# The skip of a Mamba-2 recurrence on VectorE and GpSimd instead of TensorE, the state's decay ahead of the next chunk's products, and other places for TensorE's product steps

## The reference

```python
# graph part of layer 0
msg = layernorm(x) @ W + B
sens = exp(-(1.0 / adj - 1.0) ** 2 / 0.5)
x = x + where(adj < 1.0, sens, 0.0) @ msg
# feed-forward part of layer 0: a Mamba-2 block on layernorm(x), 8 heads of 64, state 64
z, xBC, dt = split(x @ W_in);  xBC = silu(conv4(xBC) + conv_b);  xh, Bm, Cm = split(xBC)
dt = softplus(dt + dt_bias);   A = -exp(A_log)
h[t] = exp(dt[t] * A) * h[t-1] + dt[t] * outer(xh[t], Bm[t])       # per head
Y[t] = h[t] @ Cm[t] + xh[t] * D[:, None]                            # the last term is the skip
Y = Y * silu(z);  Y = Y * rsqrt(mean(Y * Y) + EPS) * norm_w
x = x + (Y @ W_out) @ W_lin + b_lin
```

## Time and profile before

| | us |
|---|---|
| median of three runs (2358.29 to 2360.41) | 2358.39 |
| span of the profiled execution | 2358.5 |
| TensorE busy (share of the span) | 2189.1 (93%) |
| VectorE busy | 1803.0 (76%) |
| ScalarE busy | 1566.7 (66%) |
| GpSimd busy | 1146.6 (49%) |
| mean granted TensorE clock | 0.979 |

### The profile page before, as it was taken

How to read it: one execution, slowest core, us unless ns; L and a number is a source line. 1 busy time by engine, 2 the same in 40 slices (tenths; PEclk the granted TensorE clock), 3 DMA queues, 4 the chain that set the end, 5 groups by cost and what they waited for, 6 DMA issues and landing times.

```text
span 2358.5 us, 26231 instructions
## 1 busy us (share of the span) xinstructions
PE 2189.1 (93%) x8900; PEld 1393.1 (59%) x8900; DVE 1803.0 (76%) x2083; ACT 1566.7 (66%) x2541; POOL 1146.6 (49%) x928
## 2 busy tenths in 40 slices
PE   7999999999999999989999999998999987787998
PEld 4544545555555556456766666676766664444886
DVE  5666767777777765324999998999989998996665
ACT  5577686777686845425676767677676868775444
POOL 2101322222231313213988888888988888890000
PEclk9999999999999999999999999999999999898999
DMA  6243332323232323233323232323323221312121
GB/s 234 72 134 102 108 116 90 125 96 122 87 125 88 119 90 134 83 107 109 131 93 125 90 125 89 117 99 107 117 100 125 90 83 43 117 36 98 36 81 45
DMA packets 117495, 241.22 MB, mean 102 GB/s; under 512 B 8770, under 2 KB 66370, under 8 KB 116978
## 3 DMA queue, kind: packets, MB, share of 16 engines
q1 hardware_dynamic: 108290, 207.14, 26.4%
q0 software_dynamic: 8528, 31.36, 3.8%
q10 hardware_dynamic: 544, 1.05, 0.1%
HBM read 219.20 MB, written 20.32 MB: 102 GB/s over the span
## 4 chain that ended last, share of the span: by engine, by line
PE 65%; ACT 10%; POOL 10%; DVE 10%; issue 5%; DMA 0%; ACTq 0%; DVEq 0%; POOLq 0%
PE ps L685 13%; PE ps L727 10%; POOL dB L2306 6%; PE ps L971 5%; DVE h L1473 3%; PE ps L849 2%; PE ps L823 2%; PE ps L955 2%; POOL acc L2288 2%; PE ps L709 2%; ACT ps L1659 2%; ACT L1657 1%; POOL du L2302 1%; PE ps L755 1%; PE ps L753 1%
## 5 line engine op out<-in xcount | busy, mean ns | idle before, releaser
L1473 DVE TENSOR_TENSOR_SCAN h<-ps,hst,dB 128x512 f32<-128x512 f32 x512 | 636.9, 1270 | 59.0 <-ACT ps L1659 50.5
L2306 POOL TENSOR_TENSOR dB<-du,bc 128x512 f32<-128x512 f32 x512 | 648.0, 1287 | 61.6 <-DVE h L1473 59.1
L685 PE MATMUL ps<-wgt,msg 128*128 128x512 f32 x1024 | 489.0, 598 | 2.1 <-DVE xb L1181 2.1
L1659 ACT ACTIVATE ps<-dt,cols 128x512 f32<-128x512 f32 x512 | 351.9, 692 | 181.1 <-DVE h L1473 178.8
L727 PE MATMUL ps<-raw,msg 128*128 128x256 f32 x1792 | 436.3, 379 | 0.9 <-ACT hb L1659 0.9
L971 PE MATMUL ps<-consts,h 128*128 128x128 f32 x2048 | 318.9, 281 | 70.7 <-DVE acc L1435 38.0
L971 PEld LDWEIGHTS ps<-consts,h 128*128 128x128 f32 x2048 | 251.6, 144 | 224.8 <-DVE acc L1435 73.4
L727 PEld LDWEIGHTS ps<-raw,msg 128*128 128x128 f32 x1792 | 324.0, 190 | 74.1 <-issue 42.1
L685 PEld LDWEIGHTS ps<-wgt,msg 128*128 128x128 f32 x1024 | 190.0, 192 | 206.2 <-issue 204.6
L1659 ACT ACTIVATE wgt<-wgt 128x1024 f32<-128x1024 f32 x256 | 257.9, 1046 | 51.9 <-DVE wgt L1146 50.5
L2288 POOL TENSOR_TENSOR acc<-acc,part 128x512 f32<-128x512 f32 x174 | 226.4, 1301 | 59.7 <-ACT part L1659 58.3
(11 more groups left out here) (320 smaller groups left out, 3589.9 us busy)
## 6 DMA issues: line engine op xcount, KB each, us to landing
raw<-in_adjT SPq DMA_DIRECT2D x256, 512.0 KB, 3.4
bc<-tmp_bc SPq DMA_DIRECT2D x64, 512.0 KB, 4.6
E<-tmp_bc POOLq DMA_DIRECT2D x32, 512.0 KB, 4.1
xb<-in_xT POOLq DMA_DIRECT2D x8, 512.0 KB, 4.1
tmp_x<-xb POOLq DMA_DIRECT2D x8, 512.0 KB, 4.2
x<-tmp_x SPq DMA_DIRECT2D x8, 512.0 KB, 5.8
tmp_x<-x SPq DMA_DIRECT2D x8, 512.0 KB, 4.8
msg<-in_W SPq DMA_DIRECT2D x4, 1024.0 KB, 10.6
```

The lines of the kernel that those rows point to most:

```text
L685: x = e.matmul(P[d][:, :], msg[:, j, d * 128:(d + 1) * 128], wgt[g % NW][:, l, :], start=j == 0, stop=j == NJ - 1)
L1473: e.tensor_tensor_scan(hr[n % 3][:, m, :], PS[4 + k % 2].t[:, :], dBr[k % 4][:, :], hst[:, n % 16, m:m + 1], ALU.mult, ALU.add).then_inc(S ...
L1659: return e.activation(out, in_, func, bias=bias, scale=scale)
L2306: e.tensor_tensor(dBr[k % 4][:, :], du[:, m, :], bcr[i % 3][:, n % 2, :], ALU.mult).then_inc(S("dB"), 1)
```

## The change

- The skip leaves TensorE. The four matmuls by diagD of each chunk are gone; the products with E now start the bank Y. In `inner(s)` VectorE first multiplies the transposed x tile X by a row of D spread over all partitions (`Drow`) into a new tile `skips[s % 2]`; in `outer(s)` GpSimd adds tmp to it (semaphore skip), and VectorE's last sum reads skips instead of tmp.
- Drow is made once, near 37 us: one more matmul on TensorE (a matrix of ones by diagD) and a copy on VectorE. diagD now shares the memory of skips[0], and the bias row Bbc that of skips[1]; the rows are loaded by two DMAs instead of one, and both are waited for.
- GpSimd's decay of the state (`carried`) no longer opens `outer(s)`. It stands in `inner(s + 1)`, ahead of xdec and of the product E for that chunk; for the last chunk it opens `outer`.
- FILLS puts 23 instead of 16 product steps at named places, and 7 fewer are spread. In the part quoted above TensorE's stream now reads: layernorm, transposes(0), p6, transposes(1), p, layernorm, p7, L745, Yo(0), p, St(0), p, Y(0), p, xbc0, p, transposes(2), p, xbc0, p2, z0, Yo(1), p, z0, St(1), sums, p, xbc1.
- The last stage counts two events on one semaphore (b2c) instead of two.

```diff
-        rows = sb(cA, "rows", [128, NROW])
-        Bbc, dtb, Abc = rows[:, 0:256], rows[:, 256:288], rows[:, 288:296]
-        diagD = sb(cA, "diagD", [128, 4, 128])
+        rows = sb(cA, "rows", [128, NROW - D])
+        dtb, Abc = rows[:, 0:32], rows[:, 32:40]
+        Drow = sb(cA, "Drow", [128, 512])
...
+        skip0 = sb(cA, "skip0", [128, 512])
...
+        skips = [skip0, sb(cA, "skip1", [128, 512])]
+        diagD = skip0[:, :].rearrange("p (m c) -> p m c", m=4)
...
-        FILLS, SEND, WFIRST, WLAST, EVAC, PREND = ((5, 3), (7, 2), (8, 2), (25, 2), (30, 2), (38, 2), (50, 2), (57, 1)), 58, 0.04, 0.925, 0.97, 0.95
+        FILLS, SEND, WFIRST, WLAST, EVAC, PREND = ((5, 3), (7, 2), (8, 3), (25, 2), (30, 2), (32, 2), (38, 4), (50, 3), (57, 2)), 58, 0.04, 0.925, 0.97, 0.95
...
-                    w.wait_ge(S("setup"), 5)
                     w.wait_ge(Y.evac, Y.n - 1)
-                    for m in range(4):
-                        e.matmul(Y.ps[:, m * 128:(m + 1) * 128], cc[:, m, ts_], diagD[:, m, :], start=m == 0, stop=False,
-                                 skip_group_check=True)
                     yield
                     w.wait_ge(S("M"), 4 * ib + s + 1)
                     w.wait_ge(X.evac, X.n)
                     for h in range(8):
-                        i = e.matmul(Y.ps[:, h * 64:(h + 1) * 64], Es[:, h, :], xd[:, h * 64:(h + 1) * 64], start=False,
-                                     stop=h == 7, skip_group_check=True)
+                        i = e.matmul(Y.ps[:, h * 64:(h + 1) * 64], Es[:, h, :], xd[:, h * 64:(h + 1) * 64], start=True,
+                                     stop=True)
...
+                    b = drow_use()
+                    w.wait_ge(S("setup"), 5)
+                    w.wait_ge(b.evac, b.n - 1)
+                    e.matmul(b.ps[:, :], one, skip0[:, :], start=True, stop=True).then_inc(b.full, 1)
...
+                    if c < 2:
+                        w.wait_ge(drow_use().evac, drow_use().n)
+                    e.tensor_tensor(skips[s % 2][:, :], X.ps[:, :], Drow[:, :], ALU.mult)
                     e.tensor_tensor(heads(xd[:, :]), heads(X.ps[:, :]), dt[:, 8 * s:8 * s + 8, None].broadcast_to([128, 8, 64]),
                                     ALU.mult).then_inc(X.evac, 1)
...
                     w.wait_ge(Y.full, Y.n)
-                    w.wait_ge(Yo.evac, Yo.n)
-                    e.tensor_tensor(tmp[:, :], tmp[:, :], Y.ps[:, :], ALU.add).then_inc(Y.evac, 1)
+                    w.wait_ge(S("skip"), c + 1)
+                    e.tensor_tensor(tmp[:, :], skips[s % 2][:, :], Y.ps[:, :], ALU.add).then_inc(Y.evac, 1)
...
+                    b = drow_use()
+                    w.wait_ge(b.full, b.n)
+                    e.tensor_copy(Drow[:, :], b.ps[:, :]).then_inc(b.evac, 1)
...
-            e.dma_start(rows[:, :], t["rows"].broadcast_to([128, NROW])).then_inc(S("d_rows"), 16)
+            e.dma_start(rows[:, :], t["rows"][:, D:NROW].broadcast_to([128, NROW - D])).then_inc(S("d_rows"), 16)
+            e.dma_start(Bbc[:, :], t["rows"][:, 0:D].broadcast_to([128, D])).then_inc(S("d_rows"), 16)
...
                     yield
+                    if s:
+                        carried(s - 1)
                     w.wait_ge(X.evac, X.n)
...
-                def outer(s):
+                def carried(s):
                     if s:
                         w.wait_ge(outer_use(ib, s - 1, 1).evac, outer_use(ib, s - 1, 1).n)
...
                     e.tensor_tensor(heads(hd[:, :]), heads(h0[0:64, :]), ecd[0:64, 2, s, :, None].broadcast_to([64, 8, 64]),
                                     ALU.mult).then_inc(S("hd"), 1)
-                    yield from [None] * 5
+
+                def outer(s):
+                    yield from (None, None)
+                    Yo = outer_use(ib, s, 0)
+                    w.wait_ge(Yo.evac, Yo.n)
+                    e.tensor_tensor(skips[s % 2][:, :], skips[s % 2][:, :], tmp[:, :], ALU.add).then_inc(S("skip"), 1)
+                    yield from (None, None, None)
```

More of the change, by code:

```diff
@@ L219, in build @@
         hd = sb(cA, "hd", [64, 512])
+        skip0 = sb(cA, "skip0", [128, 512])
+        cM = ExitStack()
+        Bbc = sb(cM, "Bbc", [128, D])
+        cM.close()
+        skips = [skip0, sb(cA, "skip1", [128, 512])]
+        diagD = skip0[:, :].rearrange("p (m c) -> p m c", m=4)
         cA.close()
@@ L283, in message_use @@
             if ib % 2:
-                return ring_b.use(ib // 2 * 6 + (4 if ib > 1 else 0) + i)
+                return ring_b.use(ib // 2 * 6 + (5 if ib > 1 else 0) + i)
             return ring_a.use(ib // 2 * 6 + i)
@@ L288, in combined_use, with drow_use @@
             return ring_b.use(6 + m)
+        def drow_use():
+            return ring_b.use(10)
         def pre_use(ib, i):
@@ L436, in build @@
         over_a = [(prod[1].use(NB).full, prod[1].use(NB).n), (ssd_use(NB - 1, 27).evac, ssd_use(NB - 1, 27).n), (ssd_use(NB - 1, 31).evac, ssd_use(NB - 1, 31).n),
-                  (S("hd"), 4 * NB), (S("M"), 4 * NB), (S("xdec"), 4 * NB), (S("halo"), NB + 1),
+                  (S("hd"), 4 * NB), (S("M"), 4 * NB), (S("skip"), 4 * NB), (S("xdec"), 4 * NB), (S("halo"), NB + 1),
                   *((S(f"d_x2_{b}"), 16 * len(range(b, NB, 3))) for b in range(3)), (S("d_m2"), 16 * (NB - 2))]
@@ L1087, in mean_of_bias @@
                 b = end_use(2)
-                w.wait_ge(S("b2c"), 1)
+                w.wait_ge(S("b2c"), 2)
                 w.wait_ge(b.evac, b.n - 1)
@@ L1134, in messages @@
                 yield
-                w.wait_ge(S("d_rows"), 16)
+                w.wait_ge(S("d_rows"), 32)
                 for s in range(4):
@@ L1138, in messages @@
                     w.wait_ge(b.full, b.n)
-                    e.tensor_tensor(msg[:, 4 * ib + s, :], b.ps[:, 0:256], Bbc, ALU.add).then_inc(b.evac, 1)
+                    e.tensor_tensor(msg[:, 4 * ib + s, :], b.ps[:, 0:256], Bbc[:, :], ALU.add).then_inc(b.evac, 1)
                     yield
@@ L1574, in second_matrices @@
                 w.wait_ge(b_tw.evac, b_tw.n)
-                e.tensor_scalar(b2[:, 0, :], b2[:, 0, :], tw[:, 0:1], None, ALU.mult).then_inc(S("b2a"), 1)
-                w.wait_ge(S("b2a"), 1)
+                e.tensor_scalar(b2[:, 0, :], b2[:, 0, :], tw[:, 0:1], None, ALU.mult).then_inc(S("b2c"), 1)
+                w.wait_ge(S("b2c"), 1)
                 e.scalar_tensor_tensor(b2c[:, :], b2[:, 1, :], tw[:, 1:2], b2[:, 0, :], ALU.mult, ALU.add).then_inc(S("b2c"), 1)
@@ L2217, in ssd @@
                         yield from inner(s + 1)
+                    else:
+                        carried(s)
                     yield from outer(s)
```

2 lines of the change are left out of this document (1 added, 1 removed).

## The result

| | before | after |
|---|---|---|
| median of the runs | 2358.34 us | 2380.64 us (2376.35 to 2382.33, 4 runs) |
| ratio | | 1.0087, 95% interval 1.0075 to 1.0099 |
| profiled span, mean granted clock | 2358.5 us, 0.979 | 2374.3 us, 0.973 |

A forecast was written before the change was run, and what follows sets the result against it. TensorE was taken to bound steady blocks (busy 110.2 of 112.4 us). Start +1.8, six blocks -7.0, seventh -2.4 and eighth -3.0 sum to -10.6 us, from 2358.39 to 2347.8; range 2332 to 2357.

The forecast's parts named there:

- forecast at 19.1 us: Second xbc group: TensorE arrives 19.1 us after the dt matmuls instead of 22.6, then waits for ScalarE's z copy.
- I take 0.6: Block start: VectorE's new product makes the normalised input late, so the dt matmuls at L745 start 0.6 us later.
- the upper bound of 1.9: Block start: the loss at L745 if the early decay on GpSimd also fell on VectorE's L1146 pair, 1.9 us.
- between 0 and 0.75 us later: First y of a block: VectorE's product with z, which ScalarE awaits, is done 0 to 0.75 us later.
- two meetings on GpSimd: First y: skip sum beside the L1146 pair, costing VectorE 0.2 to 1.3 us, and E beside L1153, possibly 2.4.
- waits until 592.95 to 593.7: Second xbc group: TensorE arrives at 591.6, waits for the z copy, starts 0.75 to 1.5 us earlier than before.
- 1.1 of gain: Steady block: wins 0.75 to 1.5 us, taken as 1.1, of the 3.56 us that TensorE saves.
- The clock: Blocks: granted clock was 1.00 despite 1.14 us idle spells; a fall would make the prediction wrong altogether; no chance given.
- Forecast 5.4 us for the two blocks: Last two blocks, where TensorE has idle time: 2.4 us won in the seventh and 3.0 in the eighth.
- the start 0.7 instead of 1.8: Kernel start: one more matmul and VectorE's copy cost 0.9 to 2.2 us, taken as +1.8.
- The 0.45 us a chunk: Eighth block: decay and update leave the chunk's cycle and the skip sum enters, a gain of 0.45 us a chunk.
- the third was nearest: Rival: VectorE and the shared access become the bound, up to 7.5 us a block against 3.56 saved; 2371 us, chance 0.10.

The follow-up runs named there:

- the new places alone: The kernel before the change with only the changed kernel's places for the product steps; 2359.61 us (0.9994 to 1.0013).
- no sum: The changed kernel without GpSimd's skip sum, VectorE's product still made but unused; median 2370.09 us, ratio 1.0037 to 1.007.
- the split with old places: The changed kernel with chunks 0 and 1's skip on TensorE, decay behind E, earlier z copy, product steps placed as before the change; 2360.77 us.

## Why the prediction was wrong

**What held.** TensorE's saving is 3.56 us a block. Its arrival at the second xbc group, forecast at 19.1 us behind the dt matmuls, was 19.24 (22.57 less the wait of 3.33). The limit there is ScalarE's z copy. The state's update no longer waits for the decay.

**The block start (step: "I take 0.6").** The product's part was right, 0.68 us, but it is the product of chunk 1, the second transpose group. What failed is the reason by which I set the upper bound of 1.9 aside: that the decay comes up while the second half of the VectorE pair is already running. It came up about then (459.69, while the second half was recorded as running from 459.40) and got in all the same. The dt matmuls waited 1.90 us, which is that bound; the decay alone costs 1.3 (1.29 in the kernel before, 1.30 in the one without skip).

**The first y (step: "between 0 and 0.75 us later").** It comes 1.46 us later, counted from dt matmuls that are 1.90 late themselves. The loss needs both the early decay and the sum, on whichever engine the sum stands: with the decay late y is 0.28 later, without the sum 0.09 earlier, with the sum on VectorE 1.47 later. I had counted two meetings on GpSimd and left out the third, the decay of the next chunk, which the edit puts beside the pair ahead of y (472.73 beside 471.23). A moved instruction has a new neighbour in every chunk, not only where its old wait was.

**The z copy (step: "waits until 592.95 to 593.7").** Forecast 1.3 to 2.1 us, measured 3.33. I let the dt matmuls slip by 0.6 and left the copy at its old time. But y is counted from the dt matmuls (10.17 before, 10.18 in the run with neither skip nor early decay), so the copy slips with them: the wait is 1.87 us without any delay of y, and the 1.46 of y come on top.

**The steady block.** 1.90 + 3.33 - 3.56 is 1.7 us of loss instead of 1.1 of gain, with the clock at 1.00. The block measured at 1.00 is 2.3 us longer (114.60 against 112.28); the other 0.6 is in pieces too small to be placed.

**The clock.** The prediction named it as what would make it wrong altogether, gave it no price and no chance. By windows of 1 us the six blocks hold six stretches at half clock, 3.4 or 6.8 us long, 27.3 us together, which cost TensorE up to 13.7 us. Added up over the six blocks: 21.4 saved, 23.9 of new waits (9.5 at L754, 14.5 at L762), 1.0 of a new wait at a group sum in the sixth (L647; the new places alone make 0.9 there), 13.7 of half clock, and 2.1 in small pieces. That is the +19.4. It doesn't mean that the kernel would be 13.7 us faster at full clock: in the blocks that began at half clock TensorE comes later to the z copy and waits 1.48 us instead of 3.33. They take 114.43 us, no more than the 114.60 of the block at 1.00; only the two of 117.5 are longer, by 2.9 each. What brings the clock down is not settled (below).

**The last part.** Forecast 5.4 us for the two blocks, measured 4.3; the start 0.7 instead of 1.8. The number is near by luck, for the reason given for the eighth block fails. By itself the early decay does shorten this part: from 150.1 to 147.5 us in the kernel before, from 145.4 to 141.0 without any skip. In the change it wins nothing, 145.8 us against 145.6 with the decay late. The 0.45 us a chunk that I counted for it (1.04 + 0.68 - 1.27) is not there while GpSimd makes the sums; with the sums on VectorE the last part takes 141.3. What shortens it by 4.5 us with the decay late, the matmuls gone or the new places, was not taken apart.

**Among the rivals** the third was nearest, VectorE and the shared access on the path. The 5.5 us a block that it put on the path is close to the 5.2 found, but not at its places: L823, L807 and the transposes had no wait, L745 and the second L753 had (L754 and L762 after). Its reason against, 28 us of idle time on VectorE a block, was worthless: the idle time lies elsewhere in the block. And the engine is not full: more sums on it made the block shorter (110.62 against 111.15 us) and the last part too (141.94 against 145.05).

## What to carry to other kernels

An instruction moved ahead on one engine is costed by all the neighbours it gets on the engines that share its memory access, in every iteration; if a bound rests on such a meeting and the only reason against it is half a microsecond of order, take the bound. Work taken off a full engine was kept here only where no chain fell due behind it: split such a change by iteration or chunk, and put the new pieces where the helping engine stands idle, here chunks 0, 2 and 3. The sum of two SBUF tiles was cheaper on the busy VectorE (0.7 us) than on the idle GpSimd (1.26 us during which VectorE can stand).

## What the runs showed of the hardware

- Which of the two gets the access isn't told by the starts in the profile. In the changed kernel the second half of the VectorE pair began at 459.4, 0.3 us ahead of the decay (459.69), and was still stretched by the whole decay, to 2435 ns. In the kernel before, the second half of the pair at 571.78 began at 572.9, 0.6 us ahead of the E product (573.48), kept its 1210 ns and held the product instead (2.86 us). Three more such meetings, ahead of the first y: begun 0.4 us ahead of the decay in the changed kernel and 0.5 ahead with the sum on VectorE, the second half was stretched (2524 and 2633 ns); begun 0.7 ahead, without the sum, it kept its 1218 ns. The two instructions by source line, first after, then before (count; duration in ns, shortest, median, longest; first and last start):

```profile
L1155 DVE SCALAR_TENSOR_TENSOR wgt<-wgt x2: 2435/2488/2542, 456.9 to 459.4; 128x1024 f32<-128x1024 f32 x2
```

```profile
L1153 DVE SCALAR_TENSOR_TENSOR wgt<-raw,wgt x2: 1209/1210/1210, 571.8 to 572.9; 128x1024 f32<-128x1024 f32 x2
```

The Trainium skill (SBUF — State Buffer, section "SBUF: two separate sides") gives the access to whichever starts first, for the whole instruction. The second half of that agrees with these rows, the first doesn't by the recorded starts.
- A 32-column VectorE instruction took 0.88 instead of 0.18 us beside a GpSimd sum (470.20, the sum 469.76 to 471.03): the price is the rest of the GpSimd instruction, for this small one as for those of 1024 columns.
- By the profiled blocks, or by the mean clock of the runs where those kept 1.00, the granted clock fell in every kernel that had a new wait of 1.3 us or more ahead of the dt matmuls, the z copy or the state's matmul, though not in each block, and not in each run (no sum: 2355.6 us at 0.980, 2366.6 to 2370.4 at 0.972 or 0.973). It stayed at 1.00 in the split with old places, with 1.83 us of idle time ahead of the transposes in each block. So the length of a single spell doesn't decide it; what does was not found out.
